# A mixture-of-experts kernel: TensorE reads the next expert's bounds inside each tile, and GpSimd and SyncE get another order

## The reference

```
t = to_tokens(x)                                   # 2048 tokens of 256
xt = layernorm(t)
gate = softmax(xt @ Wg)                            # 8 experts
topv, topi = top_k(gate, 2);  topv /= sum(topv) + 1e-6
for e in range(8):
    h  = gelu(xt @ W1[e] + b1[e])                  # 256 -> 1024
    ye = h @ W2[e] + b2[e]                         # 1024 -> 256
    out += ye * scores[:, e]                       # zero unless e is one of the token's two
t = t + out
```

## Time and profile before

| | us |
|---|---|
| median of 3 runs | 409.26 (407.37 to 410.68) |
| the profiled execution | 408.46 |
| its span, first to last instruction | 406.7 |

### The profile page before, as it was taken

How to read it: one execution, slowest core, us unless ns; L and a number is a source line. 1 busy time by engine, 2 the same in 40 slices (tenths; PEclk the granted TensorE clock), 3 DMA queues, 4 the chain that set the end, 5 groups by cost and what they waited for, 6 DMA issues and landing times.

```text
span 406.7 us, 8244 instructions
## 1 busy us (share of the span) xinstructions
PE 362.1 (89%) x2500; PEld 324.9 (80%) x2501; DVE 257.4 (63%) x650; ACT 254.4 (63%) x555; POOL 188.2 (46%) x232
## 2 busy tenths in 40 slices
PE   5989978999999796999999899898999999899950
PEld 4435456887879686899999798898989999899950
DVE  5858388788767996554467347784457854935530
ACT  2496657669557764756667466786567855865520
POOL 5800000002025655435666556685657556766553
PEclk9999999999999878999999999999999999999995
DMA  7810000000002773718325631658224714232342
GB/s 272 262 39 2 0 1 2 0 2 0 1 16 92 309 267 95 245 58 229 61 49 133 169 63 42 161 146 266 54 52 90 210 42 71 36 66 55 54 65 27
DMA packets 22965, 38.62 MB, mean 95 GB/s; under 512 B 2576, under 2 KB 17296, under 8 KB 22800
## 3 DMA queue, kind: packets, MB, share of 16 engines
q1 hardware_dynamic: 14896, 25.41, 17.9%
q0 software_dynamic: 8032, 12.82, 17.9%
HBM read 28.85 MB, written 9.37 MB: 94 GB/s over the span
## 4 chain that ended last, share of the span: by engine, by line
PE 51%; DVE 12%; POOL 12%; issue 11%; ACT 6%; DMA 3%; POOLq 2%; DVEq 1%; ACTq 0%
PE banks L1273 8%; PE banks L1275 8%; PE banks L1274 8%; PE banks L1613 5%; PE banks L1617 5%; PE banks L1615 5%; POOL xg L523 5%; POOL out_rows L573 4%; PE banks L1388 3%; PE banks L1311 3%; DMA xg<-xn_rows,idx_in 3%; ACT prob L677 2%; DVE y_out L1212 1%; PE banks L1572 1%; DVE expx L917 1%
## 5 line engine op out<-in xcount | busy, mean ns | idle before, releaser
L820 ACT ACTIVATE h_raw<-banks,b1t 128x256 f32<-128x256 f32 (+1 forms) x136 | 68.3, 502 | 76.0 <-PE banks L1275 76.0
L1221 DVE TENSOR_TENSOR h_lo<-h_raw,h_hi 128x256 fp32r<-128x256 f32 (+1 forms) x136 | 58.5, 440 | 70.8 <-ACT h_hi L823 70.0
L573 POOL DMA_INDIRECT out_rows<-y_out,idx_out x36 | 72.5, 2014 | 42.3 <-DVE y_out L1212 36.5
L1273 PE MATMUL banks<-x_hi,w_hi 128*128 128x256 f32 (+1 forms) x272 | 79.6, 293 | 7.2 <-issue 3.7
L1613 PE MATMUL banks<-w_hi,h_hi 128*128 128x256 f32 x288 | 83.5, 290 | 2.1 <-DVE h_lo L1221 2.0
L1615 PE MATMUL banks<-w_lo,h_hi 128*128 128x256 f32 x288 | 81.4, 283 | 0.0
L1617 PE MATMUL banks<-w_hi,h_lo 128*128 128x256 f32 x288 | 81.4, 283 | 0.0
L1274 PE MATMUL banks<-x_lo,w_hi 128*128 128x256 f32 (+1 forms) x272 | 78.6, 289 | 0.0
L1275 PE MATMUL banks<-x_hi,w_lo 128*128 128x256 f32 (+1 forms) x272 | 78.6, 289 | 0.0
L523 POOL DMA_INDIRECT xg<-xn_rows,idx_in x57 | 58.4, 1024 | 27.9 <-POOL idx_in L517 16.3
L823 ACT ACTIVATE h_hi<-banks,b1t 128x256 fp32r<-128x256 f32 (+1 forms) x136 | 68.2, 502 | 0.0
(11 more groups left out here) (219 smaller groups left out, 663.5 us busy)
## 6 DMA issues: line engine op xcount, KB each, us to landing
w_raw<-in_w SPq DMA_DIRECT2D x16, 1024.0 KB, 8.0
xn_rows<-xn SPq DMA_DIRECT2D x2, 1056.0 KB, 4.7
x<-in_x_tok SPq DMA_DIRECT2D x4, 512.0 KB, 5.1
out_rows<-x SPq DMA_DIRECT2D x1, 2048.0 KB, 9.3
b2b<-in_b SPq DMA_DIRECT2D x1, 1024.0 KB, 4.7
xg<-xn_rows,idx_in POOLq DMA_INDIRECT x57, 3.6
out_rows<-y_out,idx_out POOLq DMA_INDIRECT x36, 3.9
out_rows<-x POOLq DMA_DIRECT2D x1, 384.0 KB, 3.2
```

Of the source, the lines that this page charges most:

```text
L573: pool.indirect_dma_start(out_d, bass.IndirectOffsetOnAxis(ap=idx_out[:, i:i + 1], axis=0), y_out[:, i, :], None, compute_op=ALU.add).then ...
L820: act.activation(h_raw[j % RING][:, 0:w], banks[:, j % RING, 0:w], ACT.Gelu, bias=bias)
L1221: dve.tensor_tensor(h_lo[:, j, 0:w], h_raw[j % RING][:, 0:w], h_hi[:, j, 0:w].bitcast(F32), ALU.subtract).then_inc(h_split, 1)
L1273: pe.matmul(out, a_hi, b_hi, start=start, stop=False)
```

## The change

It has three parts. (1) TensorE reads the next expert's word inside every tile, after the first of the four tail pieces, and unpacks it into one of two sets of five registers after the second one. At the border between two experts only the branches and loop set-up on these registers are left. `bounds` gets a ninth entry, set by one more GpSimd memset at the start, because the last expert's tiles read one past the end. (2) GpSimd waits for `y_added`, copies the output indices and releases `y_free` before the gather of t + 2, where it did so after it. (3) From expert 3 on, SyncE holds the load of expert e until gather number (first tile of expert e - 3) + 2 has landed.

```diff
-        bounds = sb("bounds", [1, 2, E], I32)
+        bounds = sb("bounds", [1, 2, E + 1], I32)
...
             load_expert(sp, 1)
+            sp.wait_ge(bounds_ready, 2)
             for e in range(2, E):
 
-                sp.wait_ge(w_split, HJ * (e - 1))
                 if e == 2:
+                    sp.wait_ge(w_split, HJ)
                     for i in range(WIDE):
                         sp.wait_ge(first_gathered[i], 16)
+                else:
+                    first = expert_bounds(sp, e - 3)[0]
+                    sp.wait_ge(w_split, HJ * (e - 1))
+
+                    sp.wait_ge(x_gathered, (first + 2) * (16 * WIDE))
                 load_expert(sp, e)
...
+            pool.memset(bounds[:, 0, E:], 8).then_inc(consts_made, 1)
...
                 keep_scores(t + 1)
-                pool.wait_ge(scores_kept, t + 2)
-                pool.wait_ge(xg_turned, t + 2)
-                gather(t + 2)
-
 
                 pool.wait_ge(y_added, block * 16 + 16)
                 pool.tensor_copy(idx_out[:, :], row_out[:, bass.ds(t, 1), :].rearrange("p a w -> p (a w)")
                                  ).then_inc(idx_out_set, 1)
                 pool.wait_ge(idx_out_set, t + 1)
                 pool.sem_inc(y_free, 1)
+                pool.wait_ge(scores_kept, t + 2)
+                pool.wait_ge(xg_turned, t + 2)
+                gather(t + 2)
 
                 pool.wait_ge(y_weighted, t + 2)
...
-            act.wait_ge(consts_made, 14)
+            act.wait_ge(consts_made, 15)
...
-            def tile(t, e, n, width, turned_whole):
+            first_tile = [pe.alloc_register(f"first_tile{n}") for n in range(2)]
+            first_narrow = [pe.alloc_register(f"first_narrow{n}") for n in range(2)]
+            end_narrow = [pe.alloc_register(f"end_narrow{n}") for n in range(2)]
+            is_odd = [pe.alloc_register(f"is_odd{n}") for n in range(2)]
+            turned_whole = [pe.alloc_register(f"turned_whole{n}") for n in range(2)]
+
+            def load_bounds(e):
+                return pe.value_load(bounds[0:1, 0, bass.ds(e, 1)], min_val=8, max_val=264 * TMAX + 7)
+
+            def keep_bounds(word, n):
+
+                pe.reg_mov(is_odd[n], word % 8 // 4)
+                pe.reg_mov(first_tile[n], word // 256)
+                pe.reg_mov(first_narrow[n], word // 256 + word % 8 // 4)
+                pe.reg_mov(end_narrow[n], word % 256 // 8)
+                pe.reg_mov(turned_whole[n], word % 256 // 8 * (word % 4 // 2))
+
+            def tile(t, e, n, width):
...
-                turn_x(t + 1, turned_whole)
+                turn_x(t + 1, pe.snap(turned_whole[n], min_val=0, max_val=TMAX))
                 for j in range(HJ - RING, HJ):
                     layer2(t, n, j, width)
+                    if j == HJ - RING:
+                        word = load_bounds(e + 1)
+                    if j == HJ - RING + 1:
+                        keep_bounds(word, 1 - n)
...
             pe.wait_ge(bounds_ready, 2)
+            keep_bounds(load_bounds(0), 0)
+            for reg in (is_odd[1], first_tile[1], first_narrow[1], end_narrow[1], turned_whole[1]):
+                pe.reg_mov(reg, 0)
             first_turn()
             keep_busy(3, 0)
             with pe.Fori(0, E // 2) as pair:
                 for n in range(2):
                     e = pair * 2 + n
-                    t0, t1, odd, _, odd_after = expert_bounds(pe, e)
-
-                    turned_whole = pe.snap(t1 * odd_after)
-                    with pe.If(odd):
-                        tile(t0, e, n, WIDE, turned_whole)
-                    with pe.If(t1 - t0 - odd):
-                        with pe.Fori(t0 + odd, t1) as t:
-                            tile(t, e, n, 2, turned_whole)
+                    with pe.If_ne(is_odd[n], 0):
+                        tile(pe.snap(first_tile[n], min_val=0, max_val=TMAX - 1), e, n, WIDE)
+                    with pe.If_lt(first_narrow[n], end_narrow[n]):
+                        with pe.Fori(first_narrow[n], end_narrow[n]) as t:
+                            tile(t, e, n, 2)
```

More of the change, by code:

```diff
@@ L874, in _ @@
             dve.memset(ones[:, :], 1.0).then_inc(ones_made, 1)
-            dve.wait_ge(consts_made, 14)
+            dve.wait_ge(consts_made, 15)
             then(dve.tensor_scalar(k_i[:, 0:1], q_i[:, :], MBLK - 1, None, ALU.bitwise_and))
@@ L1177, in _ @@
             then(dve.scalar_tensor_tensor(flags[:, :], before[0:1, 0, 1:E + 1], 8.0, flags[:, :], ALU.mult, ALU.add))
-            dve.scalar_tensor_tensor(bounds[:, 0, :], before[0:1, 0, 0:E], 256.0, flags[:, :], ALU.mult, ALU.add
+            dve.scalar_tensor_tensor(bounds[:, 0, 0:E], before[0:1, 0, 0:E], 256.0, flags[:, :], ALU.mult, ALU.add
                                      ).then_inc(bounds_ready, 1)
-            dve.tensor_copy(bounds[:, 1, :], before[0:1, 1, 1:E + 1]).then_inc(bounds_ready, 1)
+            dve.tensor_copy(bounds[:, 1, 0:E], before[0:1, 1, 1:E + 1]).then_inc(bounds_ready, 1)
             dve.wait_ge(table_ready, 1)
@@ L1280, in _ @@
                 pe.matmul(banks[:, 7, 0:P], ones[:, :], ones[:, :], start=True, stop=True)
-            pe.wait_ge(consts_made, 14)
+            pe.wait_ge(consts_made, 15)
             def turn_rows(u):
```

## The result

| | us | ratio to before, 95% interval |
|---|---|---|
| kernel before, beside the first measurement | 407.75 (407.29 to 410.68, 6 runs) | |
| changed kernel | 415.51 (412.85 to 422.06, 6 runs) | 1.0156 [1.0107, 1.0205] |
| changed kernel, measured again (e9) | 418.01 (2 runs), before 408.50 | 1.0230 [1.0164, 1.0297] |
| predicted | 400.2 (396.5 to 404.8) | |

The prediction was wrong, in sign too. It is the rival to which it gave 0.06. Its profiled execution took 416.98 us with a span of 415.2, against 408.46 and 406.7 before.

A forecast was written before the change was run, and what follows sets the result against it. TensorE was taken to set the pace, its idle time being the loss. Terms -4.1 - 1.9 - 1.7 - 0.9 - 2.6 + 2.5 = -8.7 us took 408.46 to 399.8; 400.2 was stated, range 396.5 to 404.8.

The forecast's parts named there:

- What bounds the kernel, part 1's price: TensorE sets the pace, its idle time is the loss; tail read and unpacking cost nothing, four borders give -4.1 us.
- "borders stay" rival: At expert borders, branches and set-up outlast the sequencer's lead or tail loads eat it: 405 us, chance 0.12.
- Where a stall goes, say what is late next: At tiles 7, 11 and 14, once the borders' waits go, `x_lo` is late next: gain of 1.9 us.
- The port rival: GpSimd's scatter and later gather issues stretch beside VectorE's weight split, 0.5 us more per gather issue: 403 us, chance 0.13.
- Part 2: `y_free` ahead of the gather ends `y_out`'s wait for GpSimd and TensorE's `h_lo` waits: -1.7 us with refill.
- The slack of a plain tile: Gather of t + 2, now behind a scatter's landing, lands at 17.7 us, needed by 20.2: 2.5 us to spare.
- The -0.9 at the end: In the last tile, the new order lets the last scatter and so the end come 0.9 us earlier.
- Part 3's new stops: Held loads fall into scatters, later by +1 to +1.8 us (bounds +0.5 to +4.9); TensorE stops +2.5 us, bounds 0 and +8.
- the deciding point of 1.7: Further scatter lateness per held load, 8.7 / 5 us, from which the change would turn out slower.
- Costs of a stop: At TensorE's gaps, each costs more than its idle time: 0.25 us of refill added per gap that goes.
- Without new stops: Rival: scatters beside held loads hardly late (+0.5 us), slack absorbs it, 2 us less: 397.5 to 398 us, chance 0.12.
- The slower rival: At the `y_added` wait ahead of the gather, tiles 1, 4, 7, 8, 11: scatters +4.9 us, up to 15 us, 412 to 415, chance 0.06.

The follow-up runs named there:

- e1: Part 1 alone (bounds read in the tail) added to the kernel before: 412.94 us, ratio 1.0119.
- e8: Part 1 alone on the kernel before, with VectorE's `w_lo` work cut from 512 to 32 columns a piece from expert 2 on: 400.88 us, ratio 0.9799.
- e5: Changed kernel with part 3 undone, so parts 1 and 2 with loads not held: 405.01 us, ratio 0.9879.
- e11: Kernel before with part 1, and `y_free` released between the first and second of the gather's three DMAs: 400.61 us, ratio 0.9834.
- e6: Changed kernel with the weight loads of experts 3 to 7 cut from 2 MB to 64 KB, a test only: 398.35 us, ratio 0.9737.
- e2: Part 2 alone (`y_free` released before the gather) added to the kernel before: 410.07 us, ratio 1.0057.
- e15: Kernel before with part 1, `y_free` between a gather's first two DMAs, loads halved, second half behind a landed scatter: 398.39 us, ratio 0.9736.
- e4: Changed kernel with part 2 undone, so parts 1 and 3 with the old order on GpSimd: 411.06 us, ratio 1.0104.
- e10: Changed kernel with part 1 undone, so parts 2 and 3 without the read in the tail: 418.88 us, ratio 1.0249.

## Why the prediction was wrong, by its own steps

- **What bounds the kernel, part 1's price: right.** TensorE set the pace, and the borders' loss was its idle time. The read and the unpacking in the tail cost nothing. The sequencer's rows at the border from tile 5 to tile 6 in e9 (ns min/median/max, first and last start):

```profile
L1634 PEldq TENSOR_LOAD <-bounds x1: 300/300/300, 246.4 to 246.4; - x1
L1638 PEldq FUSED_REGOPS  x1: 250/250/250, 247.2 to 247.2; - x1
...
L1680 PEldq ALU_OP  x1: 32/32/32, 248.4 to 248.4; - x1
L1677 PEldq COMPARE_BRANCH  x1: 213/213/213, 249.1 to 249.1; - x1
```

  From the inner loop's end (248.4) to the next tile's matmuls handed over (249.85) are 1.5 us, forecast 1.6 against 2.75 before. The borders gave 3.8 us of 4.1. The "borders stay" rival is out. Tile 7 starts 0.34 us after its `x_lo`, forecast 0.3.
- **"Where a stall goes, say what is late next": incomplete for part 1.** I named `x_lo`. e1 and e8 show that with the old order `y_free` is late next, and that a VectorE backlog then feeds itself through GpSimd's stretched issues. The port rival (0.13) had the mechanism. In its own place, a later gather whose issues reach into the weight split, e9 shows it once: 2.4 us in one issue and a stop of 1.85 us, where it took 0.5 in each of three. In e1 it is the scatter's first issue. Here the Trainium skill ("SBUF — State Buffer", Who interferes with whom) cuts both ways: a VectorE instruction with two SBUF inputs contends with GpSimd's reads, but the same section infers that descriptor generation isn't touched by `tensor_tensor`. The runs decide: 6.29 us beside such instructions back to back (e1), 1.63 with their columns cut (e8).
- **Part 2: half right.** `y_out`'s waits for GpSimd fell from 7.8 us in 12 to 3.6 in 3, and e5 and e11 show that part 1 needs it. The `h_lo` waits of the earlier trace rows are gone in e5 and e6; e9 has the one of 1.65 us behind a late landing. The slack of a plain tile was sized about right: 2.5 us, where three scatters late by 4.1, 4.4 and 4.6 us made stops of 2.46, 1.33 and 3.03, so 1.6 to 3.0 us were absorbed. The -0.9 at the end came as +0.6: last matmul to end is 15.4 us in e2 and e5 against 14.8, as the last gather waits for a landing and the last scatter for the gather. e9 has 16.8. With the release in the middle it is 13.8.
- **Part 3's new stops: the step that failed.** "I take +1 to +1.8, being the same kind of transfer" for a scatter beside a held load. It is +2.4 to +4.6: five landings at 6.2, 7.9, 8.2, 8.4 and 8.0 us against 3.8, together 19.7 us, 3.9 each. The row to take was the gather's at a load's start, 8.4 us in the earlier trace rows, which I kept only as the upper bound. The bound of +4.9 was nearly the truth. Over the +1 to +1.8 that I took, 3.9 is 2.1 to 2.9 more per load, past the deciding point of 1.7 that I gave. I counted against this that the scatter's first DMA is out before the load. True at four of the five loads, and no help: the second is not, and `y_added` wants both. The phase does the rest: with the gather and scatter issued without a pause, a load released by the gather's landing (3.9 us after its last issue, 225.96 to 229.84) meets the scatter's second DMA (3.4 after it, 229.40). My sum had no term for where in the load the scatter falls.
- **Costs of a stop.** New stops cost more than their length: the 1.4 us of low clock behind each of three was in no term, and neither was the stretched gather issue, which the sum put at nothing.
- **The sum without that step came out, in part by luck.** Without new stops I had 397.5 to 398. e6, the change without the bytes, took 398.35, and e15, with another release and without the collision, 398.39. In e6 the stage is 10.6 us shorter than before (forecast 10.3), but its end is 0.6 longer and not 0.9 shorter.
- **The slower rival** said 412 to 415 and named place, queue and tiles. It came at 415.5 and 418.0, and the sign of being wrong that I had named, more than 6 us of waits for gathers, came with 10.5. The stops come to less than its 15 us, and the low clock, which it did not name, makes up for it. The chance of 0.06 was too low for a price whose bounds included the deciding point. The chances for "faster" also add up to 0.88 and not to 0.86.

The rule of turns by packet in the Trainium skill ("DMA: Bandwidth & Descriptors", Queues, rings and completion order), which I did not lean on, would give a scatter a few packets of delay. Four of the five landings, with 4.1 to 4.6 us more, are above the 1 to 3 us that I had estimated from it. How the two queues share the DMA engines within those microseconds no run resolves. (In the expert stage all transfers come from SyncE and GpSimd; "all eight engines' DMAs", ahead of the prediction, is a slip, the core has five engines.) Why VectorE's work stretches the gather's issue in one tile of e9 and not in e6 is not settled either; what the traces show is that it follows a late landing and a stop in the tile before. Nor is it settled why parts 2 and 3 together cost somewhat more without part 1 (e10) than with it.

## What to carry to other kernels

When a wait for a DMA's landing is moved ahead of another issue on the same stream, price that landing at the worst row of the trace for a transfer at a load's start. Then ask which event releases the load and what has just been issued at that moment. Parts of a change must be priced together: here 1 alone is +1.2%, 2 +0.6%, 3 nothing, but 1 with 2 is -1.2%, 1 with 3 +1.0% and 2 with 3 +2.5%. A cure for both was cheap: put the wait behind the first of three DMAs, so that the landing's lateness hides in the slack, and split the load.

## What the runs showed of the hardware that was not expected

- A scatter's DMA issued 0.5 us before a 2 MB load took 7.9 us to land, one issued 2.4 us before it 3.9. In the middle of a load the scatters of the kernel before took 5.6.
- Issue of an indirect DMA on GpSimd took 6.29 us beside VectorE's `w_lo` and `h_lo` back to back, 1.63 with `w_lo` cut to 32 columns. In e9 one DMA of a gather took 3.40 us beside them, 0.98 in the tiles before and after.
- After stops of 1.85, 2.46 and 3.03 us in e9 TensorE's granted clock was 0.5 (1.2 GHz) for 3.4 us each, and the two stretches shown above, without idle time, took 13.4 and 13.5 us and not 12.0. After stops of 1.72 (before) and 1.79 us (e9, at 204.03) it stayed at 2.4 GHz. But the length of the stop does not decide it: it also stayed at that level after stops of 1.95 and 2.39 us (e5, at 281.80 and 230.59) and 2.95 (e4, at 276.79).
